# Edge bias in the aggregation stages: added by VectorE on the way out of PSUM instead of by a matmul

## What is computed

```python
y = mish(edge_features @ W_edge.T + b_edge)     # (106250, 256), third block
msg = jax.nn.relu(x[src] + y)
agg = jax.ops.segment_sum(msg, dst, num_segments=node_features.shape[0])

msgs = support[edge_src] * edge_weight[:, None] # first block, twice
agg = jax.ops.segment_sum(msgs, edge_dst, num_segments=num_nodes)
```

## Time and profile before

| | us |
|---|---|
| median of 3 runs | 5736.12 |
| lowest, highest | 5725.0, 5741.83 |
| the profiled execution: span from first to last instruction (no other time of it is shown) | 6977.8 |
| PE busy, share of the span | 4133.3, 59% |
| POOL busy | 2925.0, 42% |
| DVE busy | 2046.0, 29% |
| ACT busy | 1510.4, 22% |
| mean granted TensorE clock | 0.654 |

### The profile page before, as it was taken

One profiled execution on the slowest core, in us unless ns is written; L12 is line 12 of the kernel. 1 busy time (PEld: TensorE's weight loads), 2 busy tenths in 40 slices (PEclk: granted clock), 3 DMA queues, 4 the chain that ended last, 5 costly groups with the idle time before them and its releaser, 6 DMA issues. The chain is left out here.

```text
span 6977.8 us, 63984 instructions
## 1 busy us (share of the span) xinstructions
PE 4133.3 (59%) x16404; PEld 3120.9 (45%) x16404; DVE 2046.0 (29%) x4123; ACT 1510.4 (22%) x1776; POOL 2925.0 (42%) x3015
## 2 busy tenths in 40 slices
PE   3676666676567666666532962655555555616990
PEld 2444444444344444434322851455555554415780
DVE  4223222222222222222441334332222323421212
ACT  1223222223223222222210101311111112301110
POOL 0555554453455554454114013166666664041005
PEclk8666666666666666666566985655555555558995
DMA  2344443343233333233203222254554553013213
GB/s 93 119 130 134 131 132 124 120 135 115 94 104 112 102 102 104 95 98 103 52 23 111 82 84 60 68 162 155 161 162 159 160 165 101 1 60 116 66 59 112
DMA packets 347713, 744.50 MB, mean 107 GB/s; under 512 B 68177, under 2 KB 196313, under 8 KB 347538
## 3 DMA queue, kind: packets, MB, share of 16 engines
q1 hardware_dynamic: 161522, 392.68, 16.4%
q0 software_dynamic: 118176, 284.72, 14.2%
q10 hardware_dynamic: 67968, 66.60, 3.0%
HBM read 521.40 MB, written 222.32 MB: 107 GB/s over the span
## 5 line engine op out<-in xcount | busy, mean ns | idle before, releaser
L565 PE MATMUL conv_pz<-conv_we,conv_edge 128*128 128x256 f32 x3360 | 1394.5, 536 | 505.5 <-issue 500.4
L446 POOL DMA_INDIRECT conv_gath<-support_table,conv_idx x840 | 811.8, 966 | 890.0 <-POOLq L55 631.2
L1410 POOL DMA_INDIRECT x_node<-node_table,x_idx x840 | 874.0, 1040 | 711.5 <-POOLq L55 460.1
L446 POOL DMA_INDIRECT conv_gath<-hidden_table,conv_idx x840 | 807.2, 961 | 868.3 <-POOLq L55 619.5
L565 PEld LDWEIGHTS conv_pz<-conv_we,conv_edge 128*128 128x128 f32 x3360 | 794.9, 258 | 795.9 <-issue 677.2
L1425 PE MATMUL x_pa<-x_hot,x_node 128*128 128x64 f32 x3360 | 755.4, 422 | 627.5 <-PEq L55 377.0
L1425 PEld LDWEIGHTS x_pa<-x_hot,x_node 128*128 128x128 f32 x3360 | 729.1, 331 | 654.1 <-issue 654.1
L556 PE MATMUL conv_ps<-conv_hot,conv_gath 128*128 128x64 f32 x3360 | 588.2, 331 | 497.4 <-issue 200.6
L556 PEld LDWEIGHTS conv_ps<-conv_hot,conv_gath 128*128 128x128 f32 x3360 | 538.3, 243 | 537.8 <-issue 412.1
L1206 ACT ACTIVATE conv_q<-conv_q 128x1024 f32<-128x1024 f32 x210 | 221.9, 1057 | 2218.0 <-ACTq L55 1919.6
L456 DVE TENSOR_SCALAR conv_q<-conv_pz 128x1024 f32<-128x1024 f32 x210 | 257.2, 1225 | 1463.2 <-DVEq L55 1214.2
(11 more groups left out here) (213 smaller groups left out, 4461.1 us busy)
## 6 DMA issues: line engine op xcount, KB each, us to landing
conv_edge<-in_edge_t SPq DMA_DIRECT2D x210, 512.0 KB
edge_mish_table<-conv_neg SPq DMA_DIRECT2D x210, 512.0 KB
x_neg<-edge_mish_table SPq DMA_DIRECT2D x210, 512.0 KB
e_rows<-expert_rows SPq DMA_DIRECT2D x114, 256.0 KB, 3.7
expert_outs<-e_outs ACTq DMA_DIRECT2D x114, 256.0 KB, 2.2
expert_rows<-conv_zeros ACTq DMA_DIRECT2D x35, 512.0 KB
expert_outs<-conv_zeros ACTq DMA_DIRECT2D x35, 512.0 KB
conv_gath<-support_table,conv_idx POOLq DMA_INDIRECT x840
```

The lines of the kernel that those rows point to most:

```text
L446: pool.indirect_dma_start(gath[s][:, j, :], None, table[:, :], bass.IndirectOffsetOnAxis(ap=idx[:, half, col:col + 1], axis=0),).then_inc( ...
L565: pe.matmul(ps_z[r][:, j, :], edge[r][:, m, j * P:(j + 1) * P], we[:, m, :], start=m == 0, stop=False)
L1410: pool.indirect_dma_start(node[s][:, j, :], None, c.t3[:, :], bass.IndirectOffsetOnAxis(ap=idx[:, half, col:col + 1], axis=0),).then_inc(g ...
```

## The change

The bias is loaded as 128 equal rows of float32. The bias matmul, the array of ones and the splitting of the bias into bf16 parts go. VectorE's `mish_begin` first adds the bias while it copies `ps_z[r]` to a new SBUF tile `z[r]`, waits for that, gives `ps_z[r]` back at once, and takes the minimum from `z[r]`. `mish_end` reads `z[r]` instead of `ps_z[r]`.

```diff
-        bias, parts, ones = bias_buffers(sb)
+        bias = sb("bias", [P, D])
+        z = [sb(f"z{r}", [P, CG, D]) for r in range(MISH)]
...
             def mish_begin(r):
                 take(dve, z_done[r])
                 dve.sem_inc(edge_free[r], 1)
-                nc.vector.tensor_scalar(q[r][:], ps_z[r][:], ZMAX, None, ALU.min).then_inc(z_ready[r], 1)
+                link(dve, nc.vector.tensor_tensor(z[r][:], ps_z[r][:], bias[:].unsqueeze(1).to_broadcast([P, CG, D]), ALU.add), neg_own)
+                dve.sem_inc(z_free[r], 1)
+                nc.vector.tensor_scalar(q[r][:], z[r][:], ZMAX, None, ALU.min).then_inc(z_ready[r], 1)
...
-                link(dve, nc.vector.scalar_tensor_tensor(neg[r][:], q[r][:], -1.0, ps_z[r][:], ALU.add, ALU.mult), neg_own)
-                dve.sem_inc(z_free[r], 1)
+                link(dve, nc.vector.scalar_tensor_tensor(neg[r][:], q[r][:], -1.0, z[r][:], ALU.add, ALU.mult), neg_own)
                 dve.sem_inc(neg_ready[r], 1)
...
-            nc.vector.memset(ones[:], 1.0)
...
-            split_bias(dve, nc, c, bias, parts, own)
...
                     for m in range(KD):
-                        pe.matmul(ps_z[r][:, j, :], edge[r][:, m, j * P:(j + 1) * P], we[:, m, :], start=m == 0, stop=False)
-                    last = pe.matmul(ps_z[r][:, j, :], ones[:], parts[:], start=False, stop=True)
+                        last = pe.matmul(ps_z[r][:, j, :], edge[r][:, m, j * P:(j + 1) * P], we[:, m, :], start=m == 0, stop=m == KD - 1)
                 last.then_inc(z_done[r], 1)
...
-        "l_be": np.broadcast_to(a["L1_gnn_b_edge"], (3, D)),
+        "l_be": np.broadcast_to(a["L1_gnn_b_edge"], (P, D)),
```

More of the change, by code:

```diff
@@ L419, in _ @@
             sp.dma_start(we[:], io["l_we"]).then_inc(w_in, 16)
-            sp.dma_start(bias[0][:], io["l_be"]).then_inc(w_in, 16)
+            sp.dma_start(bias[:], io["l_be"]).then_inc(w_in, 16)
             for r in range(MISH):
```

## The result

The changed kernel takes 5837.08 us (median of 4 runs, 5834.3 to 5842.57), the kernel before 5738.98 (5725.0 to 5741.98): ratio 1.0177, 95% interval 1.0144 to 1.0209. It is slower, as forecast, and 3 us from the forecast 5834. Its profiled execution has a time of 5842.57 us and a span of 5840.7.

What follows compares the result with a forecast made beforehand. POOL's back-to-back gathers were taken to bound the kernel: 5736 us, plus 108 for gathers held up by VectorE's SBUF operands, minus 10 at the start of the stages, gives 5834 us; range 5700 to 5935.

Steps and rivals of the forecast that it cites:

- What paces the kernel: Aggregation and message stages: POOL's back-to-back gathers pace, 30.4 us an iteration; the profile's 1250.5 us of waits are recording cost.
- TensorE's bias matmuls, nothing: Twelve bias matmuls an iteration go, 176 to 260 us over 840 of them, hidden under POOL's 30.4 us: worth nothing.
- PSUM given back early, nothing: Three product buffers, no wait of TensorE ending at VectorE's release: earlier release worth nothing.
- VectorE's longer way, even: Before the next indices: 0.9 us later by VectorE, 0.8 to 1.2 us earlier by the product without four bias matmuls.
- The new instructions' effect on POOL, 108 us: Last pass and minimum, now SBUF only, lengthen gathers: 401 us of work costs 108 us, ends 38 and 216.
- The price of 0.27 us per us: Gather time lost per us of VectorE work, taken from the message stage, applied to both minimum and last pass.
- Start of the stages, 10 us: Bias-splitting instructions before each aggregation stage's first gather go: 5.0 us each, 10 us off the path.
- The signs asked for: L446's gather mean rises from 0.96 to above 0.98 us, median near 0.947, long gathers under minimum and last pass.
- The 0.04: Rise of the gathers' mean, in us a gather, much beyond which the forecast would be wrong in size.
- The ports don't bite: Rival: SBUF operands don't hold up gathers; 5726 us, no measurable difference; chance 0.15.
- TensorE decides: Rival: TensorE's iteration exceeds POOL's, so removed bias matmuls pay; between 5550 and 5717, put at 5640 us; chance 0.15.
- The minimum locks POOL out for its whole length: Rival: each SBUF-to-SBUF minimum holds up a gather for its whole 0.70 us; 5942 us; chance 0.10.

Runs made afterwards that it cites:

- the long profile: First profile of the kernel before, unchanged: span 6977.8 us, against a median of 5736.12 us in runs without the profiler.
- the second profile: The kernel before, unchanged, profiled again in the first series: span 5739.2 us, measured 5745.84 us, ratio 1.0027.
- the later series: Second and third series of follow-up runs, on other chips: kernel before at 6839.36 and 6811.8 us; changed kernel, timed in the third only, 6637.99 us, ratio 0.9771.
- the 5.7 ms condition: Runs in which the unchanged kernel before takes 5739 to 5742 us: the main comparison and the first series.
- the version in place: Changed kernel, but the add writes its sum back to PSUM, minimum and last pass read PSUM, PSUM given back late: 5729.94 us, 0.9975 against the kernel before.
- the 6.8 ms one: Runs in which the unchanged kernel before takes 6839 and 6812 us: the second and third series.

## Why the prediction was right, and where it was not

*What paces the kernel.* Right for the timed runs. The sum of POOL's waits in the long profile (1250.5 us) foretold the length of an execution without them, and the second profile has it: 5739.2 us. The cause that I gave for the waits, the cost of recording, was wrong. Recorded executions at 5739.2 and 5840.7 us and timed runs at 6812 to 6839 us show that the condition belongs to neither recording nor kernel. Forecasting for the condition of the timed runs was the right choice; that the changed kernel was timed in it too is luck, as the later series show.

*TensorE's bias matmuls, nothing.* Right in the 5.7 ms condition: the version in place leaves them all out and comes to 0.9975. In the 6.8 ms one they are worth 121 and 185 us.

*PSUM given back early, nothing.* Not tried in the 5.7 ms condition; 102 us in the 6.8 ms one. The working rested on no wait of TensorE ending at VectorE's release. None does in these profiles either, and the release still counted, so that sign doesn't settle it.

*VectorE's longer way, even.* Right: the version in place has a longer way still, by 0.5 us a product, and its aggregation stages take 2126.9 us against 2126.5.

*The new instructions' effect on POOL, 108 us.* Right in kind and nearly in size: 5837.1 - 5729.9 = 107 us by the medians, 118 by the length of the aggregation stages. Its two halves were mis-sized against each other. The price of 0.27 us per us for both gave the last pass 70 us and the minimum 40; they measured 88 and 25. The last pass came out low because the message stage's loss was spread over L1446 and L1441: in the second profile it is L1446's alone, 102 us for 257 us of work, 0.40 per us, and the last pass pays about 0.35 (88 us for 255). The minimum's direct cost in the changed kernel, 43 us, is near the forecast; part of it comes back because fewer gathers then begin under the one-hots. That 0.27 came near for such a short instruction, for which no row had a price, is luck, and so is that the two errors nearly cancel.

The earlier trace rows were misread. I put the long gather at 906.53 down to L482, but L481 was still running when it began:

```profile
905.88 0.95 DVE L481 TENSOR_TENSOR conv_hot<-iota_sb,conv_rel 128x768 f32<-128x768 f32 x1
```

It ends at 906.83, and the gather at 907.64, 0.81 us later. The conclusion that two inputs in SBUF hold gathers up was right all the same.

*Start of the stages, 10 us.* The waits before the first gathers are 5.5 and 10.9 us shorter, 16 us instead of 10. (The list of signs says that the first gathers would come 5 us after where they would; the working above it means earlier, and earlier they are.) That the forecast is within 3 us has this in it: 118 for 108 on one side, 16 for 10 on the other.

*The signs asked for.* The gathers' mean rose from 0.957 and 0.963 to 1.031 and 1.035 us; I had asked for "above 0.98" and called a rise by much more than 0.04 wrong in size. It rose by 0.07: 123 us of longer gathers, against which stand 26.7 us of shorter waits, 16 of them before the first gathers and 10 inside the stages, where the forecast had no return. The 0.04 didn't follow from the forecast either: 108 us over 1680 gathers is 0.064 for each. The median stayed at 0.944, and the long gathers lie where they were looked for.

*The rivals.* "The ports don't bite" fell with the means. "TensorE decides" fell in the 5.7 ms condition. It is the nearest to what the 6.8 ms one shows, where leaving out TensorE's matmuls pays and its instructions stand apart with gaps. "The minimum locks POOL out for its whole length" was right as a mechanism: a gather that begins under the minimum ends 0.82 us after it. Its price was wrong. It let every minimum cost its whole 0.70 us, 147 us in all; but a gather pays only for what is left of the minimum, and only if its first or last 0.12 us falls under it. That makes 25 us.

The Trainium skill (SBUF — State Buffer, "Who interferes with whom") says that an instruction with two SBUF inputs contends only with GpSimd instructions that read SBUF. The traces agree if a gather counts as one: it takes its indices from SBUF (`conv_idx`), and only its first 0.12 us is held. The prediction counted it as descriptor generation, which the skill infers is not held up by such an instruction, and by that reading the last pass would cost nothing; it cost 88 us. The skill's other rule, that a two-port instruction and GpSimd shut each other out for the whole instruction, is borne out for this minimum in both directions, at 25 us and not the 147 of the rival.

## What to carry to other kernels

Where GpSimd issues gathers back to back, look at each VectorE instruction for where its operands lie before counting its time: moving one input of a 1.2 us instruction from PSUM to SBUF cost 0.42 us of gather each, and the same instruction with that input in PSUM cost none. To learn which instruction holds another engine up, don't go by what overlaps, but by ends: here the long gathers all ended the same 0.82 or 0.12 us after the instruction that had held them. Work taken from an engine that already waits for gathers only becomes waiting. And set a profile's span beside the timed runs before using a row of it; here they differed by a fifth, and which of the two conditions holds decides the sign of the change.

## What the runs showed of the hardware that was not expected

The same kernel took 5742 us in one series of runs and 6839 and 6812 us in two others, all steady within about 2%. In the long ones TensorE starts single matmuls 1.4 to 2.8 us apart in stretches, with nothing that the profile shows to wait for. What it is was not found. It isn't the recording, and it isn't the granted clock by itself: in the gaps no matmul runs at all. The chip is a rival that no run settles.

A VectorE instruction with two inputs in SBUF holds back a gather that begins under it until it has ended: at worst a gather takes 2.0 us instead of 0.94, and the cost is 0.42 us on average for each such instruction of 1.2 us. One that reads its one input from SBUF and writes SBUF (0.69 us for 1024 elements where nothing holds it, against 1.225 from PSUM) holds back the first and the last 0.12 us of a gather, at 0.12 us each on average. Where VectorE's only input, or one of its two, was in PSUM (the minimum, the add and the last pass of the version in place), no gather was held.
